# A gated block on one core: bias loads earlier, small DVE operations moved to ScalarE, the out weights loaded from ScalarE's queue, and one last store

## The reference

```python
def bit_linear(x, w, b):
    gamma_x = clip(max(abs(x), axis=-1), 1e-05, None)
    x_dq = clip(round(x * 127 / gamma_x), -128, 127) / (127 / gamma_x)
    gamma_w = clip(mean(abs(w)), 1e-05, None)
    w_dq = clip(round(w / gamma_w), -1, 1) * gamma_w
    return einsum('bsd,hd->bsh', x_dq, w_dq) + b

e = minimum(token_ids // 6250, 3)                      # expert of each row
h = layernorm(x)
y = (silu(h @ ctx[e].T) * (h @ ctx[e].T)) @ ctx[e]     # rows with expert e
x = x + tanh(g_xattn) * y
h = layernorm(x)
x = x + tanh(g_ffn) * bit_linear(silu(bit_linear(h, gate_w, gate_b))
                                 * bit_linear(h, val_w, val_b), out_w, out_b)
```

## Time and profile before

| | us |
|---|---|
| median of three timed runs | 309.68 (309.02 to 309.77) |
| the profiled execution | 310.04 |
| its span | 308.3 |
| PE busy | 291.8 (95%) |
| DVE busy | 261.4 (85%) |
| POOL busy | 238.5 (77%) |
| ACT busy | 219.2 (71%) |

### The profile page before, as it was taken

How to read it: one execution, slowest core, us unless ns; L and a number is a source line. 1 busy time by engine, 2 the same in 40 slices (tenths; PEclk the granted TensorE clock), 3 DMA queues, 4 the chain that set the end, 5 groups by cost and what they waited for, 6 DMA issues and landing times.

```text
span 308.3 us, 5341 instructions
## 1 busy us (share of the span) xinstructions
PE 291.8 (95%) x1438; PEld 141.0 (46%) x1439; DVE 261.4 (85%) x496; ACT 219.2 (71%) x276; POOL 238.5 (77%) x261
## 2 busy tenths in 40 slices
PE   1989999999999999999889999999999999999994
PEld 1445555544444555444334444444444444444453
DVE  5899987787988968679998999999998899888982
ACT  4959686777887746677986796668866876675650
POOL 5656854788888979936678799998989887977863
PEclk9999999999999999999999999999999999999999
DMA  6685798759997873923043635764445423543142
GB/s 261 228 314 202 271 313 305 251 120 307 336 279 189 230 218 102 292 60 109 19 92 72 121 69 119 122 151 88 107 115 119 85 68 86 119 87 82 54 102 105
DMA packets 58902, 49.10 MB, mean 159 GB/s; under 512 B 51135, under 2 KB 51135, under 8 KB 56576
## 3 DMA queue, kind: packets, MB, share of 16 engines
q1 hardware_dynamic: 54304, 35.43, 45.1%
q0 software_dynamic: 4576, 13.40, 12.5%
HBM read 28.35 MB, written 10.00 MB: 124 GB/s over the span
## 4 chain that ended last, share of the span: by engine, by line
PE 83%; DVE 7%; DMA 3%; issue 2%; POOL 2%; ACT 2%; DVEq 0%; POOLq 0%
PE banks L632 27%; PE banks L705 17%; PE banks L726 17%; PE banks L714 16%; PE banks L639 2%; DMA raw<-raw 2%; PE banks L609 1%; DMA xg<-in_x,gather_at 1%; DVE turned L1053 1%; DVE raw L1207 1%; DVE raw L1202 1%; POOL w_both L476 1%; DVE gu_sb L1102 1%; POOL out L548 1%; PE banks L745 1%
## 5 line engine op out<-in xcount | busy, mean ns | idle before, releaser
L476 POOL TENSOR_TENSOR w_both<-raw 128x1024 f32<-128x1024 f32 (+1 forms) x32 | 74.9, 2342 | 7.7 <-DVE raw L1202 6.8
L632 PE MATMUL banks<-w_both,turned 128*128 x348 | 80.0, 379 | 0.6 <-ACT turned L861 0.5
L939 ACT ACTIVATE w_both<-w_both,magic,raw 128x1024 f32 (+1 forms) x31 | 38.2, 1234 | 35.5 <-DVE raw L1221 35.5
L705 PE MATMUL banks<-tern,raw 128*128 128x512 bf16 x256 | 60.5, 379 | 1.6 <-DMA raw<-raw 1.2
L714 PE MATMUL banks<-tern,raw 128*128 128x512 bf16 x256 | 60.5, 379 | 1.3 <-DVE raw L1194 1.3
L726 PE MATMUL banks<-tern,xg 128*128 128x512 bf16 x240 | 56.1, 379 | 0.7 <-DVE raw L1230 0.7
L632 PEld LDWEIGHTS banks<-w_both,turned 128*128 128x128 f16 x348 | 34.0, 98 | 37.5 <-issue 2.3
L1194 DVE SCALAR_TENSOR_TENSOR raw<-banks,raw 128x1024 f32<-128x1024 f32 x32 | 40.8, 1276 | 4.7 <-issue 4.5
L1202 DVE SCALAR_TENSOR_TENSOR raw<-banks,raw 128x1024 f32<-128x1024 f32 x32 | 40.9, 1278 | 3.6 <-PE banks L714 3.6
L1207 DVE TENSOR_REDUCE raw<-w_both 128x1 f32<-128x1024 f32 x32 | 38.8, 1212 | 3.1 <-POOL w_both L476 2.9
L705 PEld LDWEIGHTS banks<-tern,raw 128*128 (+1 forms) x256 | 24.9, 98 | 32.1 <-DMA raw<-raw 1.4
(11 more groups left out here) (134 smaller groups left out, 420.2 us busy)
## 6 DMA issues: line engine op xcount, KB each, us to landing
raw<-in_ctx SPq DMA_DIRECT2D x4, 1024.0 KB, 6.7
raw<-in_L_ffn_gate_w SPq DMA_DIRECT2D x4, 1024.0 KB, 6.8
raw<-in_L_ffn_val_w SPq DMA_DIRECT2D x4, 1024.0 KB, 7.5
raw<-in_L_ffn_out_w SPq DMA_DIRECT2D x4, 1024.0 KB, 6.1
raw<-x_low SPq DMA_DIRECT2D x8, 257.5 KB, 3.5
raw<-x_high SPq DMA_DIRECT2D x8, 257.5 KB, 3.4
raw<-in_L_ffn_gate_b SPq DMA_DIRECT2D x1, 1024.0 KB, 5.4
raw<-in_L_ffn_val_b SPq DMA_DIRECT2D x1, 1024.0 KB, 9.5
```

Of the source, the lines that this page charges most:

```text
L476: nc.gpsimd.tensor_tensor(z[:, t % 2, 2 * D * c:2 * D * c + width], g_sb[:, c, 0:width], v_sb[:, c, 0:width], ALU.mult).then_inc(z_made, 1)
L632: last = nc.tensor.matmul(acc[:, :], a[:, k * P:(k + 1) * P], flat(w[:, bass.ds(e4 + k, 1), :]), start=(k == 0 and i == 0), stop=(k == KD ...
L705: last = nc.tensor.matmul(ring[pair][:, b, :], flat(xiT[:, bass.ds(t % 2, 1), k, :]), tern[:, k * HC + 2 * c + b, :], start=(k == 0), stop ...
L939: nc.scalar.activation(zq[:, a:b], flat(z[:, bass.ds(t % 2, 1), a:b]), ACT.Identity, scale=flat(sc[:, bass.ds(t, 1), 12:13]), bias=magic[: ...
```

## The change

- The four loads of the out weights leave SP. ACT issues them on its own DMA queue (`load_out`) at the start of slots 7, 8, 10 and 11, with the same three waits.
- SP issues the three bias loads when 12 pairs of `signed` are done, not 16.
- Of the x scales the two multiplied by gamma (columns 3 and 4) are made by one ACT operation between `x_round` and `x_unshift`, not by two DVE operations. Column 13 of the z scales is made by ACT (`out_scale`) behind `z_round`, not by DVE.
- The lower limit 1e-5 of the z maximum is no longer an operand: POOL writes it once into one more column behind each z tile (`ZROW`, `z_floor`), the maximum of the second half reads 1025 elements, and `z_max_both` and `z_gamma` become one operation.
- The last tile is still computed in two halves but stored by one `store`, which waits for both.

```diff
@@ -29,6 +29,7 @@
     XR = 11
+    ZROW = H + 8
     EARLY = 8
@@ -37,6 +38,7 @@
     EARLY_SLOT = 15
+    LOAD_SLOT = (7, 8, 10, 11)
     H_DMA = range(9, 17)
@@ -152,7 +152,7 @@
         x1_in = area(-(-XR * ROW // 8) * 8)[:, 0:XR * ROW].rearrange("p (b d) -> p b d", b=XR)
-        x_frees = 6
+        x_frees, bias_frees = 6, 12
         bias_g, bias_v, bias_o = area(H), area(H), area(D)
@@ -160,7 +160,7 @@
         area = areas_of(w_both[:, :])
-        z = area(2 * H).rearrange("p (b d) -> p b d", b=2)
+        z = area(2 * ZROW).rearrange("p (b d) -> p b d", b=2)
         zq = area(H)
@@ -268,11 +269,7 @@
                 m, q = n // 4, n % 4
-                if n == 8:
-                    sp.wait_ge(whi_made, PIECES)
-                    sp.wait_ge(w_copied, LOW_DVE)
-                    sp.wait_ge(wlo_pool, PIECES - LOW_DVE)
-                w = (gate_w, val_w, out_w)[m]
+                w = (gate_w, val_w)[m]
                 sp.dma_start(flat(raw[:, m * G + 4 * q:m * G + 4 * q + 4, :]), w[:, q * H:(q + 1) * H]).then_inc(raw_loaded[n], 16)
@@ -306,10 +303,8 @@
 
-            for i, j in enumerate(H_DMA[:-2]):
+            for j in H_DMA[:-2]:
                 turn_h(j)
-                if 8 + i < 12:
-                    load_weights(8 + i)
             sp.wait_ge(signed, x_frees)
@@ -321,7 +316,7 @@
                 load_rows(t)
-            sp.wait_ge(signed, G)
+            sp.wait_ge(signed, bias_frees)
             sp.dma_start(bias_g, gate_b.partition_broadcast(P)).then_inc(bias_loaded, 16)
@@ -342,9 +337,7 @@
             for n in range(YS):
-                sp.wait_ge(stored[n], 16 * ((TILES - 2 - n) // YS + 1))
-            for n in range(2):
-                sp.wait_ge(stored_last[n], 16)
+                sp.wait_ge(stored[n], 16 * TILES // YS)
 
@@ -497,6 +490,7 @@
                     pool.wait_ge(y_done, UNITS)
+                    nc.gpsimd.memset(z[:, :, H:H + 1], 1e-5).then_inc(z_floor, 1)
                     z_pair(0, 0)
@@ -533,21 +527,13 @@
 
-                pool.wait_ge(o_made, t + 1)
+                pool.wait_ge(o_made, t + 2 if t == TILES - 1 else t + 1)
                 if t >= YS:
                     pool.wait_ge(stored[t % YS], 16 * (t // YS))
                 row_at = x1_in[:, t % XR, TOKEN:ROW].bitcast(u32)
                 nc.gpsimd.indirect_dma_start(
                     out=out_rows, out_offset=bass.IndirectOffsetOnAxis(ap=row_at, axis=0),
                     in_=x1_in[:, t % XR, 0:D], in_offset=None).then_inc(stored[t % YS], 16)
-
-            def store_last(c):
-
-                pool.wait_ge(last_named, 1)
-                pool.wait_ge(o_made, TILES + c)
-                nc.gpsimd.indirect_dma_start(
-                    out=out_halves, out_offset=bass.IndirectOffsetOnAxis(ap=half_row[:, c:c + 1], axis=0),
-                    in_=x1_in[:, (TILES - 1) % XR, c * D // 2:(c + 1) * D // 2], in_offset=None).then_inc(stored_last[c], 16)
 
@@ -568,10 +554,8 @@
             add_bias(TILES - 1)
-            for t in range(TILES - 4, TILES - 1):
+            for t in range(TILES - 4, TILES):
                 store(t)
-            for c in range(2):
-                store_last(c)
 
@@ -882,7 +866,16 @@
             nc.scalar.activation(tanh_g[:, :], gates[:, :], ACT.Tanh).then_inc(tanh_made, 1)
+            def load_out(q):
+
+                act.wait_ge(whi_made, PIECES)
+                act.wait_ge(w_copied, LOW_DVE)
+                act.wait_ge(wlo_pool, PIECES - LOW_DVE)
+                nc.scalar.dma_start(flat(raw[:, 2 * G + 4 * q:2 * G + 4 * q + 4, :]), out_w[:, q * H:(q + 1) * H]).then_inc(raw_loaded[8 + q], 16)
+
             def slot(j):
+                if j in LOAD_SLOT:
+                    load_out(LOAD_SLOT.index(j))
                 sums = range(SUMMED[j - 1], SUMMED[j]) if j else range(0)
@@ -923,6 +916,8 @@
                                      bias=magic[:, 0:1]).then_inc(xq_made, 1)
+                nc.scalar.activation(flat(sc[:, bass.ds(t, 1), 3:5]), gam[:, 0:2], ACT.Copy,
+                                     scale=flat(sc[:, bass.ds(t, 1), 1:2])).then_inc(xs2_made, 1)
 
@@ -938,6 +933,11 @@
                                      scale=flat(sc[:, bass.ds(t, 1), 12:13]), bias=magic[:, 0:1]).then_inc(zq_made[half], 1)
+
+            def out_scale(t):
+                act.wait_ge(zs_made, t + 1)
+                nc.scalar.activation(flat(sc[:, bass.ds(t, 1), 13:14]), flat(sc[:, bass.ds(t, 1), 11:12]), ACT.Copy,
+                                     scale=out_gam[:, 0:1]).then_inc(zs2_made, 1)
 
@@ -966,6 +966,7 @@
                     z_round(t - 1, 1, start)
+                    out_scale(t - 1)
                 if not last:
@@ -998,6 +999,7 @@
             z_round(0, 1, start=True)
+            out_scale(0)
             with act.Fori(2, TILES - 3) as t:
@@ -1007,6 +1009,7 @@
             nc.scalar.activation(zi_last[:, 0:H // 2], zq[:, 0:H // 2], ACT.Identity, bias=magic[:, 1:2]).then_inc(zi_made[0], 1)
+            out_scale(TILES - 1)
             act.wait_ge(z_turned_ps[0], 1)
@@ -1180,14 +1183,12 @@
                 v.reciprocal(col(t, 2), col(t, 1)).then_inc(xs_made, 1)
-                v.tensor_scalar(col(t, 3), gam[:, 0:1], col(t, 1), None, ALU.mult).then_inc(xs2_made, 1)
-                v.tensor_scalar(col(t, 4), gam[:, 1:2], col(t, 1), None, ALU.mult).then_inc(xs2_made, 1)
 
             def pre_gate(t, c):
 
                 n = 2 * t + c
                 if c == 0:
-                    dve.wait_ge(xs2_made, 2 * (t + 1))
+                    dve.wait_ge(xs2_made, t + 1)
                 dve.wait_ge(g_done, n + 1)
@@ -1204,22 +1205,19 @@
                 dve.wait_ge(z_made, 2 * t + c + 1)
-                v.tensor_reduce(col(t, 5 + c), z[:, t % 2, 2 * D * c:2 * D * (c + 1)], AX.X, ALU.max,
+                if t == 0 and c == 1:
+                    dve.wait_ge(z_floor, 1)
+                v.tensor_reduce(col(t, 5 + c), z[:, t % 2, 2 * D * c:2 * D * (c + 1) + c], AX.X, ALU.max,
                                 apply_absolute_value=True).then_inc(zmax_made, 1)
 
 
             def z_max_both(t):
                 dve.wait_ge(zmax_made, 2 * t + 2)
-                v.tensor_scalar(col(t, 9), col(t, 5), col(t, 6), 1e-5, ALU.max, ALU.max).then_inc(z_step, 1)
-
-            def z_gamma(t):
-                dve.wait_ge(z_step, 2 * t + 1)
-                v.tensor_scalar(col(t, 11), col(t, 9), 1 / QMAX, None, ALU.mult).then_inc(z_step, 1)
+                v.tensor_scalar(col(t, 11), col(t, 5), col(t, 6), 1 / QMAX, ALU.max, ALU.mult).then_inc(z_step, 1)
 
             def z_scales(t):
-                dve.wait_ge(z_step, 2 * t + 2)
+                dve.wait_ge(z_step, t + 1)
                 v.reciprocal(col(t, 12), col(t, 11)).then_inc(zs_made, 1)
-                v.tensor_scalar(col(t, 13), col(t, 11), out_gam[:, 0:1], None, ALU.mult).then_inc(zs2_made, 1)
 
@@ -1294,7 +1292,6 @@
                     z_max_both(t - 1)
-                    z_gamma(t - 1)
                 if 2 <= t < TILES - 2:
@@ -1325,7 +1322,6 @@
             z_max_both(t)
-            z_gamma(t)
             z_scales(t)
@@ -1339,10 +1335,6 @@
             v.tensor_copy(flat(ziT[:, t % 2, G // 2:G, :]), zT_last[1]).then_inc(z_turned_last[1], 1)
-            row = x1_in[:, t % XR, TOKEN:ROW].bitcast(u32)
-            for c in range(2):
-                last = v.tensor_scalar(half_row[:, c:c + 1], row, 2.0, float(c), ALU.mult, ALU.add)
-            last.then_inc(last_named, 1)
             finish(TILES - 2)
...
```

5 lines of the change are left out of this document (2 added, 3 removed).

## The result

The changed kernel takes 313.49 us (median of the timed runs, 313.19 to 314.51), the kernel before, now with a fourth run, 309.73 (309.02 to 310.64): ratio 1.011, 95% interval 1.0079 to 1.0141. It is 3.8 us slower by the medians, 2.4 to 4.4 by the interval. The forecast was 308.2 us with a range of 306.4 to 310.5, and 0.13 for slower.

The account below looks back on a forecast made before the run. PE's own work bounds the kernel from 185 us on; before that its mid-kernel standstills, 3.6 us, can be won. Terms -1.20 - 1.1 + 0.4 + 0.45 = -1.45 on 309.68 give 308.2 us, range 306.4 to 310.5.

Parts of the forecast that it names:

- The out weights beside the transpositions: Slots 7 to 11: loads sharing the 16 engines with the h transpositions would cost 0 in sum.
- Rival C: Slots 8, 10, 11: ACT's load cuts into the transposition SP just issued, 1.3 us a slot, 311.7 us; chance 0.13.
- ACT's issue price: Slots 7, 8, 10, 11: issuing the loads delays gu_hi and what follows on ACT, +0.4 us (0 to 1.4).
- Bias loads: First gate matmul, near 131 us: earlier bias loads let turn_x(0) land sooner and PE's wait goes, -1.20 us.
- Small operations: PE's waits for DVE, 150 to 182 us: moving small DVE operations shortens them, -1.1 us (0 to 2.4).
- The last store: Kernel's tail: one whole-row store starts at the same time but lands later than a half, +0.45 us (0.4 to 2.2).
- D: Whole kernel: all of PE's waits for DVE go and ACT's issues are hidden, -3.15 us, 306.5 us; chance 0.14.

Follow-up runs that it names:

- experiment 4: Separate kernel, not the changed one: a transposition with a 1 MB load in six arrangements, alone and beside row transfers; median landings 3.0 to 9.3 us.
- E: Trial case: transposition on SP, load on ACT's queue about 1.2 us later; transposition lands in 3.2 us alone, 5.8 with row transfers.
- D: Trial case: transposition on SP, load right behind it on the same queue; transposition lands in 3.0 us alone, 5.7 with row transfers.
- Experiment 3: Changed kernel with the out weight loads on ACT's queue in slots 8 to 11, held back until behind the transposition: 313.83 us, ratio 1.0124.
- experiment 2: Changed kernel with all out weight loads on SP's queue, three about 1 us ahead of the transpositions of units 9, 11 and 12: 311.96 us, ratio 1.0025.

## Why the prediction was wrong

Of its five terms the two large gains held, the two small losses (ACT's issues, the store) did not come, and the one that was priced at 0 was worth 6 us.

- **The out weights beside the transpositions, priced at 0: the step that failed.** The prediction moved load 1 "from 72 to 67", which is when gu_hi(7), the activation written behind it, starts (67.03). That would be 1.2 us behind the transposition of unit 9. The load went out at 64.75, 1.16 us ahead of it at 65.91, and the 2.3 us between 67 and 64.75 turned the order of the two round. Before, each load stood behind its transposition on one queue, so it could not get in front; the change gave up that order. The measured price is 6.2 us in slots 9 to 12, with landings of 7.1, 7.5 and 5.7 us. It could have been asked of the program: the load's own waits are long over, so it goes out when the last of the waits written ahead of it on ACT ends, and that is the one of `h_hi` of the same unit, which the transposition needs too. That an ACT issue does not wait for the activations between, no row of before showed.
- **Rival C had the place and the sign, not the mechanism.** It named slots 8, 10 and 11, ACT's wait for the transposition ahead of its own work, and a loss that outweighs the rest, at 311.7 us. Its mechanism was a load that cuts into a transposition issued ahead. In the trials of experiment 4 that costs 0.2 us at most; in the kernel the loads stood ahead, and the slots to units 9, 11 and 12 grew by 3.4, 1.6 and 1.5 us where it counted 1.3 a slot. Its argument against itself, "the transposition starts over a microsecond ahead", was the false premise: it starts over a microsecond behind. The Trainium skill ("DMA: Bandwidth & Descriptors", Queues, rings and completion order) has an engine take turns, a packet at a time, between queues it has work for. By that rule E would be later than D in experiment 4; they are 3.2 and 3.0 us alone, 5.8 and 5.7 with the row transfers. Experiment 3 alone, with its one landing of 7.4 us, speaks for it. That C was nearer to the measured time than the forecast, 311.7 for 313.5, is in part luck.
- **ACT's issue price, +0.4: measured 0.** gu_hi(7) starts at 67.10 against 67.03, and the h_hi(9) ahead of the issue is as much later (64.53 for 64.46). The trace of before had no such issue, and the lower bound, 0, was right. But the same fact that makes it free, that the issue doesn't wait for its turn among the activations, is what puts the load ahead. The prediction used it for the price and not for the time of the load.
- **Bias loads, -1.20: right**, at 1.20 in the trace (gate matmul straight behind the last mark) and -0.40% (0.12 to 0.68) alone, 1.2 us. The loads go out at 115.76 only because all is 5.8 us late; directly behind the x_low rows (issued from 113.52 for 2.20 us), as forecast.
- **Small operations, -1.1: right in the waits, a little low in all.** The waits for DVE fell from 2.4 to 0.42 + 0.65 + 0.22 = 1.3 us, as forecast; from the gate matmul to PE's end it is 1.4 us less; alone -0.52% (0.23 to 0.80), 1.6 us. The activation of 128x1 on ACT took 0.28 us where 0.195 was assumed, and cost nothing in the total.
- **The last store, +0.45: measured about -0.1, and not to be told from 0.** From the end of DVE's last operation to the span's end it is 311.8 - 308.20 = 3.6 us, against 308.3 - 304.58 = 3.7. The longer landing came (2.7 us for 2.4), the start did not. The forecast had the single store start 0.78 us behind DVE, as the second half did. It starts 0.28 behind (308.48): the 0.78 of before was POOL issuing the first half until 304.67 and then 0.69 us of its own ("issue" in the earlier trace rows). The forecast read the start as the price of the wait ahead of it, without looking at what the engine did just before.
- **The sum.** With the measured terms: +6.2 - 1.2 - 1.4 - 0.1 = +3.5 on 310.04 gives 313.5, the time of the profiled execution. Two slips in the working change nothing: D's own sum is 306.5, not the 306.4 named as the lower end, and of the three waits put down to DVE's backlog up to 155 us the one at 158.80 lies outside that window.

Open: why the kernel with the loads on ACT's queue behind the transpositions (experiment 3) is slow and varies by 7 us between runs, where the same place on SP's queue is not and does not, and what makes up the 0.9% between experiment 2 and the changed kernel. There is no trace of one of experiment 3's longer runs.

## What to carry to other kernels

A DMA moved to another engine's queue loses the place that the old queue gave it. Before it is priced, work out when it will be issued (by its semaphores and by whichever wait written ahead of it ends last, not by when the activation behind it starts) and put that beside the issue of every short DMA on which engines wait. Here a 1 MB load about 1 us ahead cost the transposition 1.6 to 2.4 us in the trials and up to 3.9 in the kernel, the same load right behind it 0.0 to 0.2 in the trials. And follow a late DMA along the buffer that it reads: where there is one buffer, the engines that refill it form a ring with it, and here that ring, not PE, set the pace.
